# Mamba block and gated MLP on one core: first groups spread by TensorE, four step slots, D*x on ScalarE, the whole convolution on TensorE

## The reference

```python
xz = x @ W_in.T;  x_ssm, z = split(xz)              # 256 channels each
x_ssm = silu(causal_conv(x_ssm, conv_w) + conv_b)   # depthwise, 4 taps
proj = x_ssm @ W_x.T;  B, C = proj[:16], proj[16:32]
dt = softplus(proj[-1:] * W_dt + b_dt);  A = -exp(A_log)
h = exp(dt*A)*h + (x_ssm*dt)*B ;  y = sum_n h*C     # scan over 256 tokens, 16 states
y = (y + x_ssm*D) * silu(z)
x1 = layernorm(x + y @ W_out.T)
```

```python
h = silu(w1 x1) * (w2 x1);  h = gelu(h1 h);  h = gelu(h2 h)
out = layernorm(x1 + w3 h)
```

## Time and profile before

| | us |
|---|---|
| three runs | 1138.49, 1142.07, 1145.43 (median 1142.07) |
| the profiled execution | 1137.36, of which the span in the trace is 1135.6 |
| busy in the span: PE / DVE | 998.2 (88%) / 999.5 (88%) |
| busy in the span: ACT / POOL | 894.7 (79%) / 859.3 (76%) |

### The profile page before, as it was taken

The page is one execution under the profiler, slowest core; times in us unless marked ns, Lnnn a source line. Parts: engine busy times, 40 slices in busy tenths (PEclk is TensorE's granted clock), DMA queues, the critical chain, the costliest instruction groups (busy, mean ns, idle before and its releaser), DMA issues.

```text
span 1135.6 us, 12707 instructions
## 1 busy us (share of the span) xinstructions
PE 998.2 (88%) x3744; PEld 427.3 (38%) x3744; DVE 999.5 (88%) x1438; ACT 894.7 (79%) x1255; POOL 859.3 (76%) x515
## 2 busy tenths in 40 slices
PE   4346699999999998998999999999999999998897
PEld 1112234343343434344343434434343433434343
DVE  1499999999999999999999999999999999999611
ACT  4386689988888887988888998888889898887331
POOL 1276786988889796877979798888979788888640
PEclk8677699999999999999999999999999999999999
DMA  4989679494959779393977949395976939395000
GB/s 114 221 232 234 133 179 212 114 242 96 244 111 231 166 170 231 80 244 84 234 160 173 227 107 245 94 250 110 219 180 164 235 94 244 81 243 124 9 10 10
DMA packets 65845, 186.01 MB, mean 164 GB/s; under 512 B 9968, under 2 KB 29424, under 8 KB 49392
## 3 DMA queue, kind: packets, MB, share of 16 engines
q1 hardware_dynamic: 65248, 184.89, 69.7%
q10 hardware_dynamic: 528, 0.32, 0.1%
HBM read 163.15 MB, written 22.02 MB: 163 GB/s over the span
## 4 chain that ended last, share of the span: by engine, by line
ACT 48%; PE 19%; DMA 17%; issue 8%; DVE 6%; SPq 1%; POOL 1%; ACTq 0%; DVEq 0%; POOLq 0%
ACT dA L422 19%; DMA dtr<-scr_dt 13%; PE G L784 5%; PE G L762 4%; ACT L491 4%; PE G L769 3%; ACT hid L491 3%; DVE hb L659 3%; DMA xdr<-scr_xd 2%; PE Y L753 2%; ACT dts L470 2%; ACT soft L470 2%; DMA xT_sb<-xT_d 2%; ACT soft L473 2%; ACT L422 2%
## 5 line engine op out<-in xcount | busy, mean ns | idle before, releaser
L357 POOL TENSOR_TENSOR pb<-hb,crep 128x1024 f32<-128x1024 f32 x256 | 603.2, 2364 | 155.4 <-DVE hb L659 147.5
L659 DVE TENSOR_TENSOR_SCAN hb<-dA,U 128x512 f32<-128x512 f32 x512 | 594.4, 1203 | 0.0
L422 ACT ACTIVATE dA<-dtr,negA 128x510 f32<-128x510 f32 x512 | 333.6, 710 | 84.9 <-DMA dtr<-scr_dt 70.5
L652 DVE TENSOR_TENSOR U<-X,xdr 128x512 f32<-128x512 f32 x512 | 326.9, 685 | 30.9 <-DMA xdr<-scr_xd 17.9
L762 PE MATMUL G<-hid,h_sb 128*128 128x512 f32 x512 | 234.5, 602 | 21.8 <-ACT g L491 21.0
L762 PE MATMUL G<-g,h_sb 128*128 128x512 f32 x512 | 234.3, 601 | 0.0
L753 PE MATMUL Y<-pb,sel_sb 128*32 128x512 f32 x1024 | 141.6, 626 | 23.6 <-POOL pb L357 23.6
L762 PEld LDWEIGHTS G<-hid,h_sb 128*128 128x128 f32 x512 | 93.5, 190 | 160.6 <-issue 124.5
L762 PEld LDWEIGHTS G<-g,h_sb 128*128 128x128 f32 x512 | 93.3, 189 | 138.3 <-issue 136.5
L399 POOL TENSOR_TENSOR hid<-hid,g 128x512 f32<-128x512 f32 x64 | 81.0, 1276 | 26.8 <-ACT g L573 26.2
L784 PE MATMUL G<-w_sb,hid 128*128 128x128 f32 x480 | 61.9, 291 | 23.6 <-ACT hid L491 23.6
(11 more groups left out here) (99 smaller groups left out, 997.8 us busy)
## 6 DMA issues: line engine op xcount, KB each, us to landing
dtr<-scr_dt SPq DMA_DIRECT2D x64, 1024.0 KB, 9.8
xdr<-scr_xd SPq DMA_DIRECT2D x64, 1024.0 KB, 12.3
brep<-scr_rows SPq DMA_DIRECT2D x32, 256.0 KB, 10.1
crep<-scr_rows SPq DMA_DIRECT2D x32, 256.0 KB, 10.5
scr_dt<-dts SPq DMA_DIRECT2D x128, 64.0 KB, 2.5
scr_xd<-xds SPq DMA_DIRECT2D x128, 64.0 KB, 3.5
xT_sb<-xT_d SPq DMA_DIRECT2D x16, 256.0 KB, 7.2
xtok_sb<-xtok_d SPq DMA_DIRECT2D x16, 256.0 KB, 10.0
```

Of the source, the lines that this page charges most:

```text
L357: nc.gpsimd.tensor_tensor(pb[:, qs:qs + 2, :], hb[:, hs:hs + 2, :], crep[:, b % 2, g:g + 1, :].to_broadcast([P, 2, TB]), ALU.mult).then_in ...
L422: nc.scalar.activation(halves(dA[:, u % DA_RING, :])[:, :, 1:SEQ], halves(dtr[:, slot, q, :])[:, :, 1:SEQ], ACT.Exp, scale=negA[:, u:u + 1 ...
L652: nc.vector.tensor_tensor(U[i][:], X[:], xdr[:, slot, q + i, :], ALU.mult).then_inc(s_u, 1)
L659: nc.vector.tensor_tensor_scan(hb[:, 2 * (v % H_PAIRS) + i, :], dA[:, u % DA_RING, :], U[i][:], 0.0, ALU.mult, ALU.add).then_inc(s_h, 1)
```

## The change

Four things are changed.

1. In block 0 the groups k = 0, 1, 2 are not spread by DMA. PE repeats the rows with a 0/1 matrix (`replicate`, `rep_sb`): for each tile one product of 32 rows by 128 columns for dt and one for x*dt, both into the same bank BREP[q] (G0, G1, G2, Y1). The decay and U read that bank; B is read from its SBUF tile. The first product for block 1 (its x now stands in x1T) and the z products of block 0 stand behind these on PE.
2. dtr gets a fourth slot (DT_SLOTS 4, XD_SLOTS 3), so both dt groups of a channel half are issued together. soft shares the memory of xds; the order on SP's queue is another.
3. From block 1 on, `start_sum` is an ACT instruction (a copy of x_ssm into Y with the scale D), at v=0 and v=8. PE waits for it before the first sum.
4. From block 1 on, `in_conv` forms half 0 too (with wc0), at v=10; the three tap instructions of DVE at v=12 are gone, and half 1 stays at v=13. The first two gelus of h1 stand at v=11 instead of 12 on ACT.

```diff
-SLOTS = 3
+DT_SLOTS, XD_SLOTS = LOADS, 3
...
+        def by_product(b, k):
+            return b == 0 and k < 3
...
+                if by_product(b, k):
+                    act.wait_ge(s_rdt, u + 1)
...
+            def start_sum(b, c):
+                act.wait_ge(s_gate, 2 * b - 1 + c)
+                act.wait_ge(s_xs, 2 * b + 1 + c)
+                if c == 0 and b + 1 < NB:
+                    act.wait_ge(s_conv0, b + 2)
+                    act.wait_ge(s_conv1, b + 2)
+                if c == 1:
+                    act.wait_ge(s_sg, 4 * b - 1)
+                    act.wait_ge(s_upc, 4 * b - 3)
+                nc.scalar.activation(Y[c][:], xs[:, b % 2, c, :], ACT.Copy, scale=chp_sb[:, c, DP:DP + 1]).then_inc(s_start, 1)
...
+                    if v in (0, 8) and scan and j > 0:
+                        start_sum(j, (0, 8).index(v))
...
-                    if v == 12 and back:
+                    if v == 11 and back:
                         gelu(g1, 2, BH1, s_h1, s_g1, F, (0, 1))
...
+                                dve.wait_ge(s_rxd, 2 * v + i + 1)
+                                nc.vector.tensor_tensor(U[i][:], BREP[q + i], brep[:, states_of(k), :], ALU.mult).then_inc(s_u, 1)
...
-                    if v == 12 and intake:
-                        taps(I)
...
+            def replicate(e, q, x, s_o):
+                rows32 = slice(q * 2 * SD, (q + 1) * 2 * SD)
+                nc.tensor.matmul(BREP[q], rep_sb[rows32, e, :], x[rows32, 0, :], start=True, stop=True,
+                                 skip_group_check=True, tile_position=(q * 2 * SD, 0)).then_inc(s_o, 1)
...
+            pe.wait_ge(s_dt, 1)
+            for q in range(GT):
+                replicate(0, q, dts, s_rdt)
+            pe.wait_ge(s_xd, 1)
+            for k in range(3):
+                for q in range(GT):
+                    pe.wait_ge(s_dA, GT * k + q + 1)
+                    replicate(k % PARITIES, q, xds, s_rxd)
+                for q in range(GT) if k < 2 else ():
+                    pe.wait_ge(s_u, GT * k + q + 1)
+                    replicate(1 - k % PARITIES, q, dts, s_rdt)
...
                     if v == 1 and j == 0:
-                        in_conv(1)
+                        pe.wait_ge(s_u, 3 * GT - 3)
+                        pe.wait_ge(s_wc0, 1)
+                        in_conv(1, 0)
+                        pe.wait_ge(s_u, 3 * GT - 2)
+                        in_conv(1, 1)
+                        pe.wait_ge(s_u, 3 * GT - 1)
+                        z_proj(0, 0)
...
                     if v == 10 and intake:
-                        pe.wait_ge(s_xT, 16 * I + 16)
                         pe.wait_ge(s_gate, 2 * j + 1)
-                        in_proj(I)
+                        in_conv(I, 0)
```

More of the change, by code:

```diff
@@ L270, in _ @@
             spread_steps(0, 1, 0, scr_xd, xdr, s_xdr)
+            spread_steps(0, 1, 1, scr_dt, dtr, s_dtr)
+            spread_steps(0, 1, 1, scr_xd, xdr, s_xdr)
             sp.dma_start(w1_sb[:], w1).then_inc(s_weights, 16)
@@ L302, in run @@
                     store_steps(A, 0, scr_xd, xds, s_xds)
-                if front:
                     sp.wait_ge(s_dts[0], 16 * GT * (A + 1))
                     sp.wait_ge(s_dA, TILES * j + 4 * GT)
-                    spread_steps(A, 0, 0, scr_dt, dtr, s_dtr)
-                    sp.wait_ge(s_dt, 2 * A + 2)
-                    store_steps(A, 1, scr_dt, dts, s_dts)
+                    for e in range(PARITIES):
+                        spread_steps(A, 0, e, scr_dt, dtr, s_dtr)
+                    sp.wait_ge(s_store, 16 * NT * (A + 1))
+                    spread_B(A, 0)
                     sp.wait_ge(s_xds[0], 16 * GT * (A + 1))
@@ L518, in _ @@
             nc.scalar.mul(negA[:], negA[:], -1.0).then_inc(s_aneg, 1)
-            copy_z(0, 0)
-            copy_z(0, 1)
-            fill_X(0, 0)
             act.wait_ge(s_aneg, 1)
             act.wait_ge(s_zero, 3)
-            for u in range(AHEAD):
+            for u in range(2):
+                decay(0, u)
+            fill_X(0, 0)
+            for u in range(2, AHEAD):
                 decay(0, u)
@@ L553, in run @@
                         gelu(g2, 3, BH2, s_h2, s_g2, T, (2, 3))
-                    if v == (1 if back else 4) and front:
+                    if v == (1 if back else 5) and front:
                         silu_conv(A, 0)
@@ L837, in run @@
                     if v == 2 and scan:
-                        if j > 0 and front:
-                            pe.wait_ge(s_conv1, A + 1)
-                        start_sum(j, 0)
-                    if v == 2 and front:
+                        if j == 0:
+                            start_sum(j, 0)
+                    if v == (2 if back else 4) and front:
                         if tail:
@@ L853, in run @@
                         hidden(BH2[3], h2_sb, 3, g1, s_g1, s_h2, T)
-                    if v == 4 and front:
+                    if v == (4 if back else 5) and front:
                         pe.wait_ge(s_zc, 2 * A + 1)
```

198 lines of the change are left out of this document (108 added, 90 removed).

## The result

| | us |
|---|---|
| before, four runs on the same chip | 1136.05 to 1145.43, median 1140.28 |
| after, four runs | 1104.14 to 1108.54, median 1106.15 |
| ratio | 0.97, 95% interval 0.9652 to 0.9747 |
| profiled execution: before / after | 1137.36 / 1104.14, spans 1135.6 / 1102.3 |

The forecast was 1109; the kernel takes 1106.15, 34 us less than before. The two profiled executions differ by 33.2, and so do their spans. The gates of channel half 0 cut the span into four parts. A gain is the difference of the same stretch in the two traces.

A forecast was written before the change was run, and what follows sets the result against it. DVE (62.02 us busy of a 64.21 us middle block) and PE (60.86) were taken as the bound. Start 12, middle 16, block 14 to 15 0.5, end 2.5: 1137.4 - 31 = 1106.4, plus 2.6 for a median: 1109; range 1093 to 1129.

The forecast's parts named there:

- block 14 to 15: Stretch between the gates of these blocks: no taps there, only D*x moves, a gain of 0.5 us.
- PE and DVE in the middle: Middle blocks: DVE falls to 59.7 us, PE rises to 61.5 and becomes the tighter engine, floor 62.2.
- middle term: Blocks 1 to 14: 63.0 us a block against 64.2, times 13, a gain of 16 us (0 to 26).
- The queue of spreads: Middle blocks, SP's queue: xdr lands at 622.7 with no slack left; the loop through it takes 62.8 us a block.
- the mark that I set: Middle blocks: the queue step counts as wrong if DVE waits over 2 us for xdr.
- The start: Up to block 1: first U at 24.5, fourth group's at 54 instead of 65.82; 12 us gained (6 to 18).
- the prediction's lower bound: Block 0's repeat products on PE: four take 1.93 us together, 0.48 each, at 1.2 GHz, with row strips overlapping.
- block 1's xdr, now wanted earlier, 1.3: Start: DVE loses 1.3 us because block 1's xdr is wanted earlier.
- The end: From v=9 of block 15: the 2.25 us gelu wait and one D*x (1.02) go; 2.5 us kept, 1 to 3.3.
- PE was the pace already: Rival, middle blocks: all three waits for ACT stay, the block grows by 0.6 to 64.8; 1137 us; chance 0.07.
- xdr rival: Middle blocks: xdr lands behind two dt spreads at 626.3, 2.9 us more a block; 1165 us; chance 0.05.
- first rival: Start: row strips do not overlap and the clock stays low, fourth group at about 80; 1130 to 1133; chance 0.12.

The follow-up runs named there:

- e4: Changed kernel with the taps on DVE again (from block 2 on) and D*x on PE again; 1102.75 us, ratio 0.9682.
- e8: Changed kernel with the spreads in the old order and with the old waits in the middle blocks; 1140.63 us, ratio 1.0024.
- e3: Changed kernel with D*x as a product on PE again from block 1 on; 1123.48 us, ratio 0.985.
- e9: Changed kernel with taps on DVE, D*x on PE and the two gelus at v=12 again; 1111.52 us, ratio 0.9757.
- e1: Changed kernel with the first xdr spread issued ahead of the second dt spread in each block; 1105.10 us, ratio 0.9686.
- e11: Changed kernel; taps on DVE in even blocks from 2, PE convolution in odd; xdr first for block 1; block 0's ACT copies a step later; 1102.61 us.
- e12: The kernel of e11 with the first xdr spread ahead of the second dt spread in all blocks; 1105.04 us, ratio 0.9709.
- e5: Changed kernel with block 0's first three groups spread by DMA again, no rows repeated on PE; 1107.82 us, ratio 0.9713.
- e10: Kernel before with only the first two gelus of h1 moved to v=11; 1145.30 us, ratio 1.0041.

## Why the prediction was right, and where it was not

The sum of 31 us met a gain of 33 in the profiled executions partly by luck. The middle brought 9.2 us more than forecast and block 14 to 15 0.9, the start 6.1 less and the end 1.8, and these errors cancel.

**PE and DVE in the middle.** Right in its sums: PE at 61.58, blocks of 62.02 to 64.24 against a floor of 62.2, two of three waits for ACT gone in most of them (before w3 3.3 us are left of 15.8). The x1 chain stayed at 0.69, as said. The mark at which this step was to be wrong, more than 2.5 us idle, was reached in none of the 13 blocks (2.3 at most). What was wrong is the account behind it. The gain was put down to DVE's and PE's loads. e4 shows that the loads could be left as they were, and e8 that with the new loads alone nothing is gained. PE's load is a limit all the same, as e3 shows from the other side.

**What brought the gain.** The dt spread for the next block's second group is issued with the first instead of 10.1 us behind it. ACT then no longer stands 3.6 us for it, gives PE the gelus and h2's output in time, and PE gives DVE its sum in time. The prediction named that wait as the source of PE's waits, and then gave it no term of its own. e8 takes it back and loses everything, e9 keeps it alone (with the start) and has five sixths. This is shown for the early spreads as a whole; the fourth slot and the order were not tried apart. The traces speak for the order. By the code of before, a slot is free for this spread once ACT has formed the 28th tile of the block, here the second of these four, done at 607.43:

```profile
606.11 2.54 ACT L422 ACTIVATE dA<-dtr,negA 128x510 f32<-128x510 f32 x4
```

The spread went out at 615.74, so for 8.3 us it stood for its turn in SP's queue and not for room. In e1 it goes out at 459.36, when that tile was done (459.33): a time at which three slots would have done, and e1 has all of the gain.

```profile
459.36 0.59 SPq L256 DMA_DIRECT2D dtr<-scr_dt  x1
```

What the fourth slot gives beyond that, for the dt spreads of half 1 above all, stays open.

**The size of the middle term.** 16 us were forecast, 25.2 measured. I set a typical block of 64.2 against one of 63.0. Two blocks of before, of 67.12 and 66.84, lie 2.9 and 2.6 over it, 5.5 together, and both hold a w3 product at the lower clock:

```profile
446.97 5.33 PE L784 MATMUL G<-w_sb,hid 128*128 128x128 f32 x32 [2.63 <-ACT hid L491]
...
513.71 5.44 PE L784 MATMUL G<-w_sb,hid 128*128 128x128 f32 x32 [2.24 <-ACT hid L491]
```

where the earlier trace rows have 3.81 after 1.24. After has no such product in these 13 blocks. The prediction gave the mean of 64.71 and did not use it. The rest is the block: 62.77 on average, not 63.0.

**The queue of spreads.** The landing was forecast at 17.1 us after the first dt issue and came at 17.8; the loop through it was put at 62.8 and the period is 62.77. By the mark that I set (a wait over 2 us) this step failed in most blocks, 33.4 us in 13. The mark was badly chosen: e1 removed the wait and DVE stood for PE instead. Whether the loop through the spread would hold the block by itself is not shown. In e11 PE's mean load is lower, the wait for xdr stays (20.2 us) and the block is no shorter, which agrees with it, and as well with blocks that are held by their own fuller engine. Why e12, with the xdr wait gone too, still takes 62.81 stays open: late dt is back in ACT (14.3 us) and passes on to PE and DVE, but no run separates it from DVE's own 727.0 busy of 750.

**The start.** Mis-sized: 12 against 5.9. Its first steps held. The row strips overlapped, as the prediction's lower bound had it; PE of after, the first products (G and Y are the banks):

```profile
20.45 0.70 PE L859 MATMUL G<-dts,g 32*128 32x512 f32 x3 [3.77 <-DVE dts L676]
20.47 0.69 PE L859 MATMUL Y<-dts,g 32*128 32x512 f32 x1
20.95 0.63 PE L859 MATMUL G<-dts,g 32*128 32x512 f32 x3
21.00 0.59 PE L859 MATMUL Y<-dts,g 32*128 32x512 f32 x1
```

Eight records, four products, begin within 0.6 us and are done by 21.6: 1.1 us for the set, at the full clock (PEclk 1.00 over it), where the forecast had 1.93 at 1.2 GHz. From 22.2 to 46.0 us PEclk is 0.51, the lower level as forecast, and the sets still kept up with DVE, whose pairs of U stand 3.4 to 3.6 us apart. The first U ran at 25.63 (24.5 forecast), the fourth group's at 54.30 (54). So 11.5 us were won by then, against 65.82. The gate of block 0 still held all of that, 68.05 against 79.56. Before had no wait of DVE between the two gates but 0.97 at the second; after lost 5.6 of the 11.5 there, and its waits are: 2.59 us for ACT, busy without a gap from 55 to 81 with the SiLUs and softplus (1 was allowed), 3.84 for block 1's xdr (1.3 allowed), issued at 79.91 and 16.3 us under way, and 1.72 at the gate. The step that failed most is "block 1's xdr, now wanted earlier, 1.3": the spread waits for block 1's front, which the products at the start do not make earlier (block 1's first dt stores go out at 74.32, without the products, in e5, at 74.68). Nor were the 11.5 us all of the products' making. e5 has none of them, starts its first U at 36.62, 1.7 us later than before, and reaches the gate of block 0 6.3 us earlier: before's 8.09 us for block 1's first product and the 2.31 us of taps behind it are gone there, and 2.4 us for xdr have come. So the products brought 5.3 us at that gate and 2.5 at the next, and 3.4 of the 5.9 came from the rest of the change.

**The end.** 0.7 instead of 2.5. The step that failed is that the gelu wait of 2.25 us and one D*x would go. The wait is still there, at 1.89:

```profile
1025.74 3.70 PE L817 MATMUL G<-hid,h_sb 128*128 128x512 f32 x8 [1.89 <-ACT g L529]
```

The runs also show which part brought the 0.7. In e10, the kernel before with the earlier gelu alone, the end takes 87.05 us, and in e3 and e4, with D*x on PE, 87.08 and 87.07; in e9, without the earlier gelu, 87.76 as before. So it is the gelu's, and moving D*x gave nothing here. Behind its last gate each kernel takes 58.6 us; the difference is DVE's wait at that gate, 7.94 before and about the same in after as in e10:

```profile
1043.71 0.69 DVE L655 TENSOR_TENSOR gT<-Y,zs 128x512 f32<-128x512 f32 x1 [7.23 <-PE Y L808]
```
```profile
1080.93 0.69 DVE L612 TENSOR_TENSOR gT<-Y,zs 128x512 f32<-128x512 f32 x1 [7.24 <-PE Y L753]
```

PE's time goes there to h2, and the sum comes behind it.

**The rivals.** "PE was the pace already" describes e8 and not after: the waits stay and the block grows when the spreads stay late. Its 1137 and the 1165 of the xdr rival are counted from 1142, the forecast's 1109 from 1140; from the same base they are 1135 and 1163. In the first rival 27 + 45 + 10 is 82 and not 80, 16 us later than now. It fell with the overlap of the strips. The rival on the xdr spread wanted a landing later than 19.9 us after the first dt issue (625.5 less 605.64); it was 17.8.

## What to carry to other kernels

Two engines near full load can both be held by a third that is not: before adding up what the loads become, follow each wait of the full engines back until an engine waits for a transfer, and give that transfer a term of its own. Undo the parts of a change one at a time before crediting any of them, then undo the one nobody doubts; here taps, gelu and first groups could each be undone for 2.1 us or less, D*x alone cost 17 us, and the one part with no arithmetic in it, undone, took all of the gain away. Undoing alone isn't enough either: the gelu was worth nothing clear of the noise on top of the two moves, and 8.8 us without them. A wait that appears at a nearly full engine has no price until it has been taken away and the time has fallen.

## What the runs showed of the hardware

TensorE's granted clock fell from 2.4 to 1.2 GHz for a few us in the middle of a run in which PE was busy nine tenths of the time. In e8 the w3 product comes after waits of 2.18 to 2.77 us in every block, and in six of the twelve up to 925 us it runs slow. Two of them, the first without the fall:

```profile
182.02 3.81 PE L840 MATMUL G<-w_sb,hid 128*128 128x128 f32 x32 [2.67 <-ACT hid L530]
248.44 5.44 PE L840 MATMUL G<-w_sb,hid 128*128 128x128 f32 x32 [2.76 <-ACT hid L530]
```

Two stretches around the second (PEclk is the third number from the end):

```profile
246.80:250.20 3.40, 1.76 (x11) 1.79 (x12) 3.40 (x5) 3.36 (x5) 2.46 (x2) 0.83 1.05 213
250.20:253.60 3.40, 3.40 (x22) 3.40 (x22) 3.40 (x5) 2.44 (x5) 2.37 (x1) 0.67 1.09 235
```

The first has PE idle for about half. By the two means the clock was at the lower level for a third of the first and two thirds of the second. The product takes 1.6 us longer. The blocks concerned take 66.0 to 68.0 us where the others take 64.5 to 65.4. In these middle blocks before has two such w3, e10 three (5.16 to 5.44 after 2.28 to 2.76); after, e1 and e9 have none, and none of their waits there is longer than 1.85. Waits of 2.04 in before, of 2.17 in e12 and of up to 2.77 in e8 and e10 passed without a fall. In block 14 w3 waits 2.86 us or more in every kernel, 3.27 in after, and takes 5.16 to 6.71, but 3.81 in e3 after 2.89. So a gap of some 2.2 to 2.8 us ahead of w3 went with a fall in some blocks and not in others, and in e8 a fall cost the block about as much again as the gap.

A spread of 1 MB took 7.2 us to land where the dt spread before it was 1.7 us from its own landing, and 15.9 behind two others and B. The forecast for that queue, the bytes at the 233 GB/s of the earlier trace rows (14.6 us) and the 2.4 us by which the same sum fell short in the old order, was 0.7 us under the 17.8 measured from the first issue.
